# Causal attention of a decoder on one core: the order of ScalarE's copies within a step

## The reference

```python
q = split_heads(x @ Wq + bq)        # 16 heads of width 8
k = split_heads(x @ Wk + bk)
v = split_heads(x @ Wv + bv)
att = jnp.einsum('bhqd,bhkd->bhqk', q, k) * scale
att = jnp.where(mask, att, -inf)    # causal
att = jax.nn.softmax(att, axis=-1)
y = jnp.einsum('bhqk,bhkd->bhqd', att, v)
return y @ Wo + bo                  # x = x + this, x normalised before
```

## Time and profile before

| | us |
|---|---|
| median of three runs (lowest, highest) | 2061.98 (2061.15, 2062.81) |
| the profiled execution, its own time | 2060.05 |
| its span, first to last instruction | 2058.3 |
| TensorE busy in it | 1887.7 (92%) |
| ScalarE busy in it | 883.6 (43%) |
| the causal stage in it, scores of step 0 to the last addition | about 1325 to 1522 |

### The profile page before, as it was taken

The page is one execution under the profiler, slowest core; times in us unless marked ns, Lnnn a source line. Parts: engine busy times, 40 slices in busy tenths (PEclk is TensorE's granted clock), DMA queues, the critical chain, the costliest instruction groups (busy, mean ns, idle before and its releaser), DMA issues. The chain is left out here.

```text
span 2058.3 us, 46276 instructions
## 1 busy us (share of the span) xinstructions
PE 1887.7 (92%) x18242; PEld 1378.5 (67%) x18242; DVE 1251.9 (61%) x2923; ACT 883.6 (43%) x1679; POOL 679.1 (33%) x797
## 2 busy tenths in 40 slices
PE   4999999989999999999999999378978999999877
PEld 2566666667888888887666678256656777777643
DVE  5566666637676766666342222278856777777667
ACT  1433334445555555555322133166633444444334
POOL 2111111103333333333225300466503444444436
PEclk9999999999999999999899999699989999999999
DMA  8000000000000000000100022201100000000001
GB/s 286 1 2 0 0 0 0 1 1 1 1 1 0 0 0 0 0 0 1 72 17 23 26 71 103 58 25 24 20 2 1 2 1 0 0 0 1 2 11 31
DMA packets 31331, 40.35 MB, mean 20 GB/s; under 512 B 5225, under 2 KB 25501, under 8 KB 30708
## 3 DMA queue, kind: packets, MB, share of 16 engines
q1 hardware_dynamic: 27124, 31.97, 4.7%
q0 software_dynamic: 4096, 6.83, 1.6%
HBM read 28.30 MB, written 12.06 MB: 20 GB/s over the span
## 5 line engine op out<-in xcount | busy, mean ns | idle before, releaser
L154 POOL TENSOR_TENSOR rstd<-var_eps,minus_half 128x2 f32<-128x2 f32 (+1 forms) x116 | 92.7, 799 | 434.6 <-DVE var_eps L148 395.1
L975 POOL TENSOR_TENSOR xa_probs<-xa_probs,xa_total 128x512 f32<-128x512 f32 x128 | 133.3, 1041 | 196.5 <-DVE xa_total L1041 191.9
L1046 DVE TENSOR_REDUCE xa_top<-ps 128x4 f32<-128x512 f32 x128 | 88.0, 688 | 120.6 <-PE ps L819 119.5
L478 ACT ACTIVATE la_hid<-ps,pack_moe 128x512 f32<-128x512 f32 x128 | 87.8, 687 | 144.4 <-PE ps L310 143.3
L931 ACT ACTIVATE xa_probs<-xa_probs 128x512 f32<-128x512 f32 x128 | 80.7, 631 | 157.2 <-DVE xa_probs L1049 157.2
L2127 PE MATMUL ps<-ba_inT,pack_latent 128*128 128x256 f32 x512 | 142.0, 405 | 3.0 <-ACT ba_inT L2245 1.4
L808 PEld LDWEIGHTS ps<-xa_kvT,xa_qk_fold 128*128 128x128 f32 x512 | 96.5, 190 | 64.2 <-issue 41.6
L819 PE MATMUL ps<-xa_kvT,xa_qT 128*128 128x128 f32 x1024 | 135.3, 275 | 0.0
L835 PE MATMUL ps<-xa_probsT,xa_kv 128*128 128x512 f32 x256 | 133.3, 602 | 2.1 <-ACT xa_attnT L940 1.8
L310 PE MATMUL ps<-la_h2T,pack_moe 128*128 128x512 f32 x256 | 131.5, 628 | 0.4 <-ACT la_hid L478 0.4
L808 PE MATMUL ps<-xa_kvT,xa_qk_fold 128*128 128x256 f32 x512 | 130.7, 380 | 0.2 <-ACT xa_kvT L898 0.2
(11 more groups left out here) (312 smaller groups left out, 4181.3 us busy)
## 6 DMA issues: line engine op xcount, KB each, us to landing
expert_weights<-experts_dram SPq DMA_DIRECT2D x8, 768.0 KB, 4.5
slot_rows<-zeros SPq DMA_DIRECT2D x1, 2560.0 KB
expert_rows<-slot_rows SPq DMA_DIRECT2D x8, 320.0 KB, 3.0
result_rows<-ex_result SPq DMA_DIRECT2D x8, 320.0 KB, 2.4
pack_moe<-moe_dram SPq DMA_DIRECT2D x1, 2312.0 KB
pack_latent<-latent_dram SPq DMA_DIRECT2D x1, 2050.0 KB, 20.4
pack_latent<-biased_dram SPq DMA_DIRECT2D x1, 2048.0 KB, 8.8
out_dram<-X SPq DMA_DIRECT2D x8, 256.0 KB, 2.3
```

Of the source, the lines that this page charges most:

```text
L154: pool.tensor_tensor(m.rstd[:, 0:tiles], m.var_eps[:, 0:tiles], m.minus_half[:, 0:tiles], ALU.pow).then_inc(sem.rstd, 1)
L478: act.activation(hid[:, n // F0 % 2, n % F0, :], HIDDEN[n % 2], ACT.Silu, bias=w["b1"][:, n:n + 1]).then_inc(hid_ready, 1)
L975: pool.tensor_tensor(probs[:, u % 4], probs[:, u % 4], over(total[:, u % 4], 2, KEYS), ALU.mult).then_inc(probs_ready, 1)
L1046: dve.tensor_reduce(top[:, s % 4], scores, AX.X, ALU.max).then_inc(top_ready, 1)
```

## The change

ScalarE's list in the body of a step is written in another order; nothing is added or removed, and the lists of the other engines stay as they are. Before: copies of the queries, of the values, of the keys, then both turned halves of unit 0. After: queries, keys, first turned half, values, second turned half.

```diff
-                def copy_turned(step, u):
-                    reach(act, attn_done, count(step, UNITS, u - 1))
-                    for b in range(2):
-                        act.wait_ge(probs_turned, count(step, 2 * UNITS, 2 * u + b + 1))
-                        act.activation(probsT[:, u, b].rearrange("p j n -> p (j n)"), bank(TURN_BANK), ACT.Copy)\
-                            .then_inc(probsT_ready, 1)
+                def copy_turned(step, u, b):
+                    if b == 0:
+                        reach(act, attn_done, count(step, UNITS, u - 1))
+                    act.wait_ge(probs_turned, count(step, 2 * UNITS, 2 * u + b + 1))
+                    act.activation(probsT[:, u, b].rearrange("p j n -> p (j n)"), bank(TURN_BANK), ACT.Copy)\
+                        .then_inc(probsT_ready, 1)
...
                     if before:
-                        copy_turned(later(step, -1), 1)
+                        copy_turned(later(step, -1), 1, 0)
+                        copy_turned(later(step, -1), 1, 1)
...
                     if ahead >= 1:
                         copies_q(later(step, 1), 1 - k)
-                    if here:
-                        spread_v(step, k)
                     if ahead >= 1:
                         copies_k(later(step, 1), 1 - k)
                     if here:
-                        copy_turned(step, 0)
+                        copy_turned(step, 0, 0)
+                        spread_v(step, k)
+                        copy_turned(step, 0, 1)
                         exp(step, 1)
```

## The result

| | before | changed |
|---|---|---|
| median of five runs, us | 2061.98 (2061.15 to 2064.35) | 2054.14 (2051.89 to 2056.75) |
| profiled execution, us | 2060.05 | 2054.14 |
| span, us | 2058.3 | 2052.3 |
| ratio, 95% interval | | 0.996 (0.9945 to 0.9974) |

The account below looks back on a forecast made before the run. Bound: the causal stage's loop through ScalarE's copies, second turned half, exponential and TensorE. Gains of 9.8 us (steps 0 to 13) plus steps 14 and 15 make 10.8, less 0.5: 2061.98 - 10.3 = 2051.7 us, range 2049.7 to 2054.0.

Parts of the forecast that it names:

- step 0: Cold first step of the causal stage: rows ready at about the same distance, so the usual 0.70 us gain.
- signs of being wrong: Causal stage: step 10.0 us or less, rows pair L161 often above 0.6 us, or TensorE waiting for value copies.
- The loop that bounded the kernel: Causal step of 10.92 us: ScalarE's copies, second turned half, exponential, TensorE's work up to the next value projection.
- What is late next: Behind the second turned half, TensorE waits until about 1415.35 for VectorE's normalised rows; value copies end earlier, at 1414.84.
- The rival with values as the bound: Value copies, started 1.07 us later, delay turning the rows if slowed to 0.75 us each: 2075.5 us; chance 0.04.
- The term 0.70 us per step: Causal step shrinks from 10.92 to about 10.22 us; steps 0 to 13 gain 14 x 0.70 = 9.8 us.
- The allowance of 0.5 us for GpSimd: Taken off the gain for two or three late steps where GpSimd's addition slows the normalised rows, up to 0.41 us each.
- the whole wait goes: Normalised rows not in the way: step is ScalarE's new loop, 10.01 us, 13.6 us saved, 2048.4 us; chance 0.13.
- a meeting in every step: VectorE's rows and GpSimd meet each step, rows 0.41 us late: 0.29 us saved per step, 2057.6 us; chance 0.12.
- The wider reading: A gather's issue on GpSimd also holds the shared port: each step would lose what a meeting in every step loses.

## Why the prediction was right, and where it was not

The mechanism was right: which wait goes, and which takes its place. The size was not. Inside the stage the sum promised 10.3 us and 4.7 came; the missing 5.6 are, rounded, 2.0 in steps 1 to 8, 2.6 in steps 9 to 12, 0.7 in step 0 and 0.2 in steps 13 and 14. One of the signs of being wrong that were written down did come: the pair of rows took longer than 0.6 us in 8 of 14 steps (0.62 to 1.32).

**The loop that bounded the kernel** was as read: with the keys in ScalarE's idle time TensorE's 0.91 us before the second turned half went (15.1 us to 1.4, two waits of 0.69 at the start of the stage). The two copies moved as placed: the second half starts 1.62 us after the first (forecast 1414.42 - 1412.73 = 1.69).

**What is late next** was as read: the normalised rows, not the value copies, with VectorE's wait for scores down from 1.68 and 1.39 us in alternate steps to 1.26 and 0.94, by 0.43 where 0.7 was forecast. The rival with values as the bound did not come: only in step 0 did TensorE wait for them, 0.21 us.

**The term 0.70 us per step was mis-sized**, it is 0.45 in steps 1 to 8, which cost 2.0 us. Two distances behind the new wait were taken from rows in which TensorE had not waited. From the end of the rows to their turning it is 0.13 us (1411.85 to 1411.98) where I took 0.06. From that to the products of the scores it is 1.14 (1411.98 to 1413.12) in one step and 1.01 (1422.43 to 1423.44) in the next, where I took 0.96 from 1415.82 to 1416.78. With the distances before and behind these, 10.45 us come out where I wrote 10.22, and 10.34 in every other step. That TensorE went on less tightly behind the new wait than in the rows I took the distances from is what I left out; why it does so is not shown. The run without gathers, in which nothing lengthens the rows, gains 0.49 us a step in steps 1 to 8, so this has cost about 1.7 of the 2.0 us. The other 0.3 are in steps 2 to 4, where the rows took 0.65 to 0.79 us beside the issue of a gather (below).

**The allowance of 0.5 us for GpSimd was mis-sized**: steps 9 to 12 gained nothing, forecast 2.3. The mechanism was named, and the run without gathers gives its size in these steps, 2.0 us where 0.5 was taken off; the rest of what is missing there, about 1 us, is the 0.70 again. What I did not follow up is the loop that I had the rows for. From the combine's start to the end of the four issues it is about 7.9 us, plus the time until the last gather has landed. Before the change the last issue ahead of the combine in the earlier trace rows ended at 1474.27, 3.95 us before that combine started, which makes the loop 11.8 us there, longer than the 10.2 I gave the step, so the combine had to fall back a little each step and into the rows. It was visible before the change as a wait of GpSimd that cost nothing.

**Step 0 gained nothing**, forecast 0.7. TensorE was granted the lower of its two clock levels for longer, until 9.6 us after the first maximum, before until 7.2: its scores of unit 1, which started 6.98 us after that maximum in both, took 1.26 us in the changed kernel and 0.79 before, and the first turned half started 0.9 us later. In the seven other profiled executions on chips that do not stall, all with the new place of the keys, the lower level lasted until 7.5 to 10.0 us and these scores took 1.25 or 1.26 in six, 0.96 in one. Both kernels are the same up to there, so the order of the copies did not do it directly; why only the kernel before came up so early, in its one execution, is open.

**The rival "the whole wait goes"** was wrong for this change, and nearly right as the next bound: it gave ScalarE's loop 10.01 us, and where the rows were taken out of the way steps went at 9.89 to 10.23.

**The rival "a meeting in every step"** had the right price, 0.41 us, but it took a delay of GpSimd of 1.4 us to bring it about, and then not in every step.

**On the page cited** ("SBUF — State Buffer" of the Trainium skill, section "SBUF: two separate sides"): its lock agrees with the pairs of 0.9 to 1.46 us beside GpSimd's additions and weighings. The instruction that was held ended 0.08 us behind GpSimd's, at 1476.51 against 1476.43 in the worst step above and at 1481.16 against 1481.08 in the earlier trace rows. The page limits the lock to some kinds of VectorE instruction, which the prediction left out; no run here varies the kind.

The wider reading, that the issue of a gather holds the rows too, I had dismissed, and it is right for a part of the issue. The changed kernel, step 3, with no addition or weighing near:

```profile
1379.62 1.03 POOL L1880 DMA_INDIRECT ca_got<-result_rows,ca_slot  x1 [0.16 <-issue]
1379.89 0.79 DVE L161 TENSOR_SCALAR ca_xn<-X,mean_var,rstd 128x128 f32 x2
```

The second instruction of this pair took 0.53 us in place of 0.34. In all kept traces together, 29 instructions of this kind began 0.45 to 0.64 us after the start of an issue, with nothing else of GpSimd beside them: all took longer, 0.38 to 0.58 us, and ended 1.0 to 1.05 after the issue's start. The 51 that began in its first 0.4 us took 0.34. The pair at 1414.70 before misled me: its first instruction took 0.41, but the second ran beside it and the pair had its usual length. In the kernel with one gather ahead and the rows early, the rows are finished 0.3 us after the issue starts, so that run says nothing against it; and without gathers every pair took 0.59 or 0.60. How the issue holds VectorE is not shown.

## What to carry to other kernels

Before a wait is taken away in a hand-pipelined loop, write down the other loops through the same engine with their lengths, and count in each the queues that have waited without cost so far: here a gather loop that grew to 11.8 us lay hidden behind a step of 10.9. An engine that idles for one input while another lies ready is worth a swap in its list; measure each half of such a change alone, since here one of two was all of it. And moving work ahead on a queue is safe only once everyone who waits for what is thereby moved back has been named.

## What the runs showed of the hardware that I had not expected

- Gathers of equal size land later and later within the stage. In the changed kernel the last issue of a set ended at 1471.26, and the combine that waited for it started at 1475.39, 4.1 us later; the first set that a combine waited for in the middle of the stage was 2.4 us behind its last issue (1405.71 to 1408.10), and no combine waited for the sets between the start of the stage and that one. But a set issued ahead of the stage, until 1325.90, was waited for until 1334.70, 8.8 us. Why is open.
- The issue of a gather holds up VectorE's normalised rows, but only those that begin about half a microsecond after its start (above).
- On some chips TensorE stops in its own list within this stage, waiting for nothing that the profile shows, and is granted the lower clock level again and again: from 1340 to 1500 us the mean granted clock was 0.79 to 0.90 in the five profiles there, 0.98 in the kernel before and the changed kernel elsewhere. A stretch of one attend in the changed kernel there; 16 such matmuls ran through in 0.43 us elsewhere:

```profile
1432.14 0.32 PE L1737 MATMUL ps<-ca_probsT,ca_vheads 128*32 128x64 f32 x3 [0.46 <-issue]
1432.89 0.33 PE L1737 MATMUL ps<-ca_probsT,pack_later_constants 128*32 128x64 f32 x5 [0.44 <-issue]
...
1435.83 0.26 PE L1737 MATMUL ps<-ca_probsT,pack_later_constants 128*32 128x64 f32 x1 [1.13 <-issue]
```

  Most steps up to step 12 take 12 to 19 us there, and the kernel before takes 2128 us. Gains of a few tenths of a us per step are not what such a chip measures; the change was worth 0.07% on it, inside its interval of no change. The cause was not tried.
